# A masked attention kernel: adjacency turned into saturated integer codes in place, and node order restored by strided accesses

## The reference

```
h      = maximum(layernorm(x), 0)
scores = where(adj > 0, (h @ weight) @ input.T, -2**32 + 1)
out    = x + softmax(scores / 0.07, axis=1) @ input
```

## Time and profile before

| What | Value |
|---|---|
| median of 3 runs | 926.37 us |
| span of the profiled execution, first to last instruction | 922.5 us |
| its own time | not given; the median is 3.9 us above the span |
| PE busy (matmul) | 906.1 us, 98% |
| PE weight loads | 659.9 us, 72% |
| DVE busy | 814.5 us, 88% |
| ACT busy | 744.0 us, 81% |
| POOL busy | 705.6 us, 76% |
| DMA | 242.46 MB, mean 263 GB/s |
| issue to landing, median | adjacency chunk 5.3 us, `pT_dma` 3.5 us |

### The profile page before, as it was taken

The page is one execution under the profiler, slowest core; times in us unless marked ns, Lnnn a source line. Parts: engine busy times, 40 slices in busy tenths (PEclk is TensorE's granted clock), DMA queues, the critical chain, the costliest instruction groups (busy, mean ns, idle before and its releaser), DMA issues.

```text
span 922.5 us, 26099 instructions
## 1 busy us (share of the span) xinstructions
PE 906.1 (98%) x7566; PEld 659.9 (72%) x7566; DVE 814.5 (88%) x1626; ACT 744.0 (81%) x1468; POOL 705.6 (76%) x587
## 2 busy tenths in 40 slices
PE   7989999999999999999999999999999999999997
PEld 4466777777777777777777777777777777777776
DVE  6998889988998899889988998898889888988985
ACT  5987888888888888888888888888888888888885
POOL 5999878787778877887788778877887788788712
PEclk9999999999999999999999999999999999999999
DMA  9789999999999999999999999999999999999965
GB/s 343 232 224 257 279 267 278 257 287 266 286 278 267 272 273 273 267 272 273 276 273 267 269 274 274 275 260 276 276 268 265 276 274 278 260 270 269 278 105 100
DMA packets 360361, 242.46 MB, mean 263 GB/s; under 512 B 321808, under 2 KB 340368, under 8 KB 341904
## 3 DMA queue, kind: packets, MB, share of 16 engines
q1 hardware_dynamic: 353136, 238.87, 100.9%
q10 hardware_dynamic: 7200, 3.28, 1.5%
HBM read 160.50 MB, written 3.15 MB: 177 GB/s over the span
## 4 chain that ended last, share of the span: by engine, by line
PE 93%; DVE 2%; DMA 2%; SPq 2%; issue 1%; ACT 0%; DVEq 0%; ACTq 0%
PE ps_s L900 38%; PE ps_o L948 26%; PE ps_o L950 13%; PE ps_t L923 13%; DMA pT_dma<-split 2%; SPq L353 1%; PE ps_t L967 1%; DVE probs L695 1%; PE ps_s L977 1%; DMA nodes_raw<-in_L_gnn_input_dram 0%; DVE v L763 0%; DVE pT_lo L718 0%; DVE split L724 0%; PE ps_o L967 0%; DVE pT_hi L714 0%
## 5 line engine op out<-in xcount | busy, mean ns | idle before, releaser
L695 DVE CUSTOM_DVE_ANT_0 probs<-ps_s,absent 128x1024 f32<-128x1024 f32 x288 | 351.4, 1220 | 49.6 <-PE ps_s L900 42.8
L900 PE MATMUL ps_s<-yT_hi,hT 128*128 128x512 f16 x1152 | 389.2, 379 | 1.0 <-DVE chunk_max L695 0.9
L460 POOL TENSOR_SCALAR absent<-present 128x2048 bf16<-128x2048 bf16 x141 | 294.3, 2087 | 34.9 <-POOL present L451 34.3
L587 ACT ACTIVATE pT_hi<-ps_t 128x512 f16<-128x512 f32 x281 | 167.7, 597 | 156.0 <-PE ps_t L923 155.9
L451 POOL TENSOR_SCALAR present<-adj_i 128x2048 bf16<-128x2048 int32 x144 | 273.6, 1900 | 13.3 <-DMA adj_i<-in_adj_dram 13.3
L948 PE MATMUL ps_o<-v,pT_dma 128*128 128x256 f16 x1152 | 222.1, 273 | 5.2 <-DMA pT_dma<-split 2.9
L557 ACT ACTIVATE ps_t<-probs,neg_max,exp_scale 128x512 f32<-128x512 f32 x285 | 220.3, 773 | 2.6 <-DVE neg_max L705 1.2
L900 PE MATMUL ps_s<-yT_lo,hT 128*128 128x512 f16 x576 | 218.3, 379 | 0.0
L718 DVE TENSOR_TENSOR pT_lo<-ps_t,pT_hi 128x512 f16<-128x512 f32 x284 | 194.3, 684 | 21.8 <-ACT pT_hi L587 20.4
L948 PE MATMUL ps_o<-v,pT_hi 128*128 128x256 f16 x1152 | 205.9, 273 | 0.9 <-DVE pT_lo L718 0.8
L950 PE MATMUL ps_o<-v,pT_dma 128*128 128x128 f16 x1152 | 206.5, 220 | 0.0
(11 more groups left out here) (82 smaller groups left out, 508.8 us busy)
## 6 DMA issues: line engine op xcount, KB each, us to landing
adj_i<-in_adj_dram SPq DMA_DIRECT2D x144, 1024.0 KB, 5.3
pT_dma<-split SPq DMA_TRANSPOSE x288, 3.5
nodes_raw<-in_L_gnn_input_dram SPq DMA_DIRECT2D x6, 512.0 KB, 6.7
x_res<-in_x_dram SPq DMA_DIRECT2D x48, 64.0 KB, 3.9
out_dram<-fin ACTq DMA_DIRECT2D x48, 64.0 KB, 2.5
x_ln<-in_x_dram SPq DMA_DIRECT2D x46, 64.0 KB, 5.0
hT<-h_split SPq DMA_TRANSPOSE x45, 5.0
x_ln<-in_x_dram ACTq DMA_DIRECT2D x2, 64.0 KB, 3.0
```

Of the source, the lines that this page charges most:

```text
L460: nc.gpsimd.tensor_scalar(by_block(absent[:, c, :]), by_row(flags(s, c)), -ABSENT, ABSENT, ALU.mult, ALU.add).then_inc(absent_done, 1)
L587: nc.scalar.activation(pT_hi[:, p % BANKS, :], turn_area(k, at), ACT.Copy).then_inc(hi_done, 1)
L695: nc.vector.tensor_tensor_reduce(out=probs[:, s, j * SCORE:(j + 1) * SCORE], in0=ps_s[j % 2][:, :], in1=absent[:, c, part * SCORE:(part + ...
L900: made = nc.tensor.matmul(ps_s[j % 2][:, q * 512:(q + 1) * 512], hT[:, s, part, :], y[:, cols], start=(part == 0 and y is yT_hi), stop=(pa ...
```

## The change

The flags and `absent` go. One pass on GpSimd (`convert`) reads a chunk as int32 and writes it over itself as uint32: 2^39 - 2^40*adj, which saturates to the largest uint32 for no edge and to 0 for an edge. The mask subtracts these codes; the scales of h and y are lowered so that scores are small beside them. Since the pass is in place, adjacency stays in the natural order of nodes, and so do scores and `probs`. The block order that `v` needs is restored elsewhere: `nodesT` is written with a step of 4 fp32 elements (16 bytes), and TensorE's transposes (as weights), `exp_d` and `split_d` read `probs` with that step.

A chunk's buffer is now free only when its last mask is done, so each load waits for `masked`. For tile 1, chunks 0 and 1 have a buffer of their own, `adj_x`, and are loaded at the start.

```diff
-    H_SCALE = 2.0 ** 12
-    Y_TOP = 14
+    H_SCALE = 2.0 ** -3
+    Y_TOP = 3
...
-    ABSENT = 2.0 ** 64
+    PRESENT_STEP = -2.0 ** 40
+    ABSENT = 2.0 ** 39
...
-        absent = sb("absent", [P, CONVS, CONV], bf16)
-        present = sb("present", [P, 2, CONV], bf16)
+        adj_x = sb("adj_x", [P, 2, CONV], int32)
...
-        def by_block(part):
-            return part.rearrange("q (g b p) -> q g b p", b=PER_TURN, p=P)
-        def by_row(part):
-            return part.rearrange("q (g p b) -> q g b p", b=PER_TURN, p=P)
+        def adjacency(u, c):
+            return adj_x[:, c, :] if isinstance(u, int) and u == 1 and c < 2 else adj_i[:, c, :]
+        def codes(u, c):
+            return adjacency(u, c).bitcast(uint32)
+        def by_row(turn):
+            return turn.rearrange("q (p b) -> q b p", b=PER_TURN)
+        def by_block(turn):
+            return turn.rearrange("q (b p) -> q b p", b=PER_TURN)
...
             def load_adj(u, c):
-                sp.dma_start(adj_i[:, c, :], adj_v[u][:, c * CONV:(c + 1) * CONV]).then_inc(adj_in[c], 16)
+                landed = adj_x_in[c] if isinstance(u, int) and u == 1 and c < 2 else adj_in[c]
+                sp.dma_start(adjacency(u, c), adj_v[u][:, c * CONV:(c + 1) * CONV]).then_inc(landed, 16)
+
+            def next_adj(u, c):
+                sp.wait_ge(masked, u * SCORES + (PER_CONV * (c + 1) - SCORES * (2 if isinstance(u, int) and u == 2 and c < 2 else 1)))
+                load_adj(u, c)
...
             sp.dma_start(x_res[:, 0, :], x_v[0]).then_inc(x_res_in[0], 16)
+            for c in range(2):
+                load_adj(1, c)
             for u in range(2, 4):
                 sp.wait_ge(h_done, u - 1)
                 load_x(u, u % 2)
-            def early_adj(n):
-                sp.wait_ge(present_done, n + 1)
-                load_adj(n // CONVS + 1, n % CONVS)
-            for n in range(2 * CONVS - 1):
-                early_adj(n)
+            next_adj(1, 2)
+            for c in range(2):
+                next_adj(2, c)
...
                     turn_d(t, 2, g, late(at, 0, g) if at == LAST else evac(t, g - 2))
-                next_adj(0)
+                if has(at, 2):
+                    next_adj(t + 2, 2)
                 for g in range(2):
                     turn_d(t, 4, g, late(at, 1, g) if at == LAST else evac(t, 2 + g))
-                next_adj(1)
...
+                if has(at, 3):
+                    next_adj(t + 3, 0)
                 if has(at, 1):
                     for g in range(2):
                         turn_d(t + 1, 0, g, late(at, 2, g) if at == LAST - 1 else evac(t, 6 + g))
-                next_adj(2)
...
                     sp.dma_start(x_res[:, s, :], x_v[t + 1]).then_inc(x_res_in[s], 16)
+                if has(at, 3):
+                    next_adj(t + 3, 1)
...
-            def find_present(u, s, c):
...
-                nc.gpsimd.tensor_scalar(flags(s, c), adj_i[:, c, :], 1.0, 0.0, ALU.min, ALU.max)\
-                    .then_inc(present_done, 1)
...
-                nc.gpsimd.tensor_scalar(by_block(absent[:, c, :]), by_row(flags(s, c)), -ABSENT, ABSENT,
-                                        ALU.mult, ALU.add).then_inc(absent_done, 1)
...
+            def convert(u, c):
+                if isinstance(u, int) and u == 1 and c < 2:
+                    pool.wait_ge(adj_x_in[c], 16)
+                else:
+                    pool.wait_ge(adj_in[c], u * 16 + (0 if c < 2 and not (isinstance(u, int) and u == 0) else 16))
+                pool.sem_inc(pool_waited, 1)
+                nc.gpsimd.tensor_scalar(codes(u, c), adjacency(u, c), PRESENT_STEP, ABSENT, ALU.mult, ALU.add)\
+                    .then_inc(coded, 1)
...
-                nc.gpsimd.tensor_scalar(split[:, d, 0, :], part, 1.0, 1.0, ALU.mult, ALU.mult)\
+                nc.gpsimd.tensor_scalar(by_block(split[:, d, 0, :]), by_row(part), 1.0, 1.0, ALU.mult, ALU.mult)\
...
-                nc.scalar.activation(part if n is None else ps_t[n % BANKS][:, :], part, ACT.Exp,
+                nc.scalar.activation(part if n is None else by_block(ps_t[n % BANKS][:, :]),
+                                     part if n is None else by_row(part), ACT.Exp,
...
-            def early_absent(u, c):
...
-                nc.scalar.activation(nodesT[:, k * TURN:(k + 1) * TURN], nodes_bank[k % 2], ACT.Copy)\
+                nc.scalar.activation(by_row(nodesT[:, k * TURN:(k + 1) * TURN]), by_block(nodes_bank[k % 2]), ACT.Copy)\
...
+                dve.wait_ge(coded, u * CONVS + (c + 1))
...
-                    in0=ps_s[j % 2][:, :], in1=absent[:, c, part * SCORE:(part + 1) * SCORE],
+                    in0=ps_s[j % 2][:, :], in1=codes(u, c)[:, part * SCORE:(part + 1) * SCORE],
...
+                rows = by_row(probs[:, par, (k + 2) * TURN:(k + 3) * TURN])
                 for b in range(PER_TURN):
-                    col = (k + 2) * TURN + b * P
-                    made = nc.tensor.transpose(area[:, b * P:(b + 1) * P], probs[:, par, col:col + P],
-                                               ident[:, :])
+                    made = nc.tensor.transpose(area[:, b * P:(b + 1) * P], rows[:, b, :], ident[:, :])
```

More of the change, by code:

```diff
@@ L21, in gnn_masked_attention_kernel @@
     fp32 = mybir.dt.float32
-    bf16 = mybir.dt.bfloat16
     fp16 = mybir.dt.float16
     int32 = mybir.dt.int32
+    uint32 = mybir.dt.uint32
     ALU = mybir.AluOpType
@@ L135, in gnn_masked_attention_kernel @@
         minus_half = sb("minus_half", [P, 1], fp32)
-        absent_top = sb("absent_top", [P, 1], fp32)
         stats = sb("stats", [P, 2, 6], fp32)
@@ L184, in gnn_masked_attention_kernel @@
         adj_in = [sem(f"adj_in{i}") for i in range(CONVS)]
+        adj_x_in = [sem(f"adj_x_in{i}") for i in range(2)]
         stored = [sem(f"stored{i}") for i in range(2)]
@@ L188, in gnn_masked_attention_kernel @@
         half_done = sem("half_done")
[L189 to L192, removed]
+        coded = sem("coded")
         stats_done = sem("stats_done")
@@ L495, in _ @@
             for c in range(CONVS):
-                if c == 2:
-                    pool.wait_ge(absent_done, 1)
-                convert(0, 0, c, False)
-            pool.wait_ge(absent_done, 2)
-            find_present(1, 1, 0)
-            pool.wait_ge(absent_done, 3)
-            find_present(1, 1, 1)
-            make_absent(1, 1, 0, True)
+                convert(0, c)
+            for c in range(2):
+                convert(1, c)
             v_lo_pool(0)
-            pool.wait_ge(absent_done, 4)
-            find_present(1, 1, 2)
-            make_absent(1, 1, 2, True)
+            convert(1, 2)
             make_h(2, 0)
-            find_present(2, 0, 0)
+            convert(2, 0)
             v_lo_pool(1)
-            find_present(2, 0, 1)
+            convert(2, 1)
             v_lo_pool(2)
@@ L518, in step @@
                     if at != 0:
-                        convert(t + 2, par, 1, True)
+                        convert(t + 2, 1)
                 if has(at, 3):
@@ L523, in step @@
                 if has(at, 2):
-                    convert(t + 2, par, 2, True)
+                    convert(t + 2, 2)
                 if has(at, 3):
-                    convert(t + 3, 1 - par, 0, True)
+                    convert(t + 3, 0)
                 if at == LAST - 1:
@@ L593, in y_hi @@
                                      scale=y_scale).then_inc(y_hi_done, 1)
-            def early_absent(u, c):
-                act.wait_ge(present_done, u * CONVS + c + 1)
-                act.wait_ge(masked, u * SCORES + (PER_CONV * (c + 1) - SCORES))
-                nc.scalar.activation(by_block(absent[:, c, :]), by_row(present[:, (u + c) % 2, :]), ACT.Identity,
-                                     bias=absent_top[:, :], scale=-ABSENT).then_inc(absent_early_done, 1)
             for u in range(2):
@@ L633, in step @@
                 for z in range(CYCLES):
-                    if at == 0 and z > 0:
-                        early_absent(2, z - 1)
                     hi_p(t, CYCLE * z, at)
@@ L685, in mask @@
                 c = j // PER_CONV
-                if isinstance(u, int) and (u, c) in ((1, 1), (2, 0), (2, 1)):
-                    dve.wait_ge(absent_early_done, u + (1 if (u, c) == (2, 1) else 0))
-                elif isinstance(u, int) and u < 2:
-                    dve.wait_ge(absent_done, u * CONVS + c + (0 if (u, c) == (1, 2) else 1))
-                else:
-                    dve.wait_ge(absent_done, u * CONVS + (c - 2))
+                dve.wait_ge(coded, u * CONVS + (c + 1))
                 dve.wait_ge(scores_made, u * SCORES + (j + 1))
```

27 lines of the change are left out of this document (1 added, 26 removed).

## The result

The changed kernel takes 1028.4 us, the median of 4 runs (1027.6 to 1035.5), beside 926.2 for the kernel before on the same chip: 1.1126 times the time, 95% interval 1.109 to 1.116. That is 102 us slower. It lies inside the range of 926 to 1056, but the likeliest time, 932, is 96 us off. That the range held the result is luck.

What follows compares the result with a forecast made beforehand. PE, busy for all 18.42 us of a period, was taken as the bound. Span 922.5 + 4.1 + 1.0 + 0.5 + 0.2 + 0.2 = 928.5, plus 3.9 to the median, gave 932 us; 8-of-10 range 926 to 1056.

Steps and rivals of the forecast that it cites:

- The DMA order in the loop: SP's queue in the loop: pairs of transposes behind loads still land in time, slack 1.5 and 1.1 us; 0, narrowly.
- Rival (b): Loop: transposes by DMA land late, 0.5 us per third, 69 us, to 1001; chance 0.08 including mixtures.
- The weights' step: TensorE's transposes reading probs as weights at a 16-byte step: no cost, hidden behind the moving operand; taken as 0.
- Rival (a): TensorE's transposes: the stepped weight load sets the pace, 0.105 us more each, 121 us, to 1053; chance 0.30.
- ACT: Loop: stepped exp_d reads up to 0.43 us longer, ACT at most 17.7 of 18.42 us; 0, by narrow cover.
- The node copies: Prologue, ACT's 12 stepped writes of nodesT: between 0 and 5 us, taken as 0.5 us.
- GpSimd: Two passes per chunk become one of 2.0 us; busy time falls some 280 us, near 420; 0 on the time.
- The mask: DVE's mask with a 4-byte instead of 2-byte second operand: still 1220 ns, no change.
- The prologue: Three loads ahead of the first transposes: PE waits 4.1 us more, plus 1.0 for lower clock and second wait.
- The likeliest case's own range: Whole kernel: bounds of the forecast's own terms around 932, given as 927 to 942 us.
- the second wait: PE's prologue wait of 2.26 us ending at 52.22, which may shrink as DVE's v products catch up.
- What would show it: Profile signs: period 18.4 us, four transposes in 0.61 us or about 0.93, no PE waits for pT_dma in the loop.

Runs made afterwards that it cites:

- experiment 5: The kernel before, with only the loop's adjacency loads waiting for the mask and issued right ahead of the pairs of transposes: 1043.5 us, ratio 1.1275.
- experiment 6: The changed kernel, with each loop load of adjacency issued between the two transposes of a pair, steps kept: 1018.1 us, ratio 1.097.
- experiment 3: The kernel before, with the 16-byte step in TensorE's transposes (weights) alone: 947.8 us, ratio 1.0245.
- experiment 4: The kernel before, with the 16-byte step in exp_d alone: 926.2 us, ratio 1.0009.
- experiment 10: The changed kernel, steps kept, with loop loads issued behind the pairs and one load instead of three ahead of the first transposes: 952.4 us, ratio 1.031.
- experiment 8: The changed kernel without steps (nodes in natural order), loop loads behind the pairs, one load ahead of the first pair, x_ln before tile 1's loads: 926.4 us.
- experiment 1: The changed kernel, with transposes and exp_d reading contiguously instead of with 16-byte steps, same issue order: 1040.9 us, ratio 1.124.

## Why the prediction was right or wrong

**The DMA order in the loop, taken at 0 "narrowly": this is the step that failed,** and it is 71 of the 96 us missed. The prediction worked out when transfers move and land, and found a slack of 1.1 us. It left the issue of a pair at the 2.8 us of the earlier trace rows, whatever stands ahead. Close behind a load a pair takes 4.6 to 4.9 us on SP, which does nothing else meanwhile. The slack of 1.1 us was no cover for three times 1.9 us in one list, since the lateness stays in the list: a pair issued late makes the next load late, and that the next pair. Its sentence "a delay doesn't pile up" was the false one. The sign of it stood in the trace of before, in a place that the text looked at only for its products. SP's queue in the prologue of the kernel before, behind the earlier trace rows:

```profile
41.95 0.58 SPq L322 DMA_DIRECT2D adj_i<-in_adj_dram  x1
42.74 4.90 SPq L353 DMA_TRANSPOSE pT_dma<-split  x2
```

A load, a pair 0.8 us behind it, and 4.90 us to issue the pair, of which SP waited for nothing: the line of the operation in this stretch reads

```profile
L353 SPq DMA_TRANSPOSE pT_dma<-split x2: 1232/2365/3498, 42.7 to 44.1; - x2
```

It is the pattern that the change makes three times a period, priced in full, and pairs of over 4 us come in that trace up to 226 us (experiment 5). Three pairs at 4.9 with the rest of the list (1.2 + 0.4 + 0.4 + 3 x 0.35, and gaps of some 3 us as the changed kernel has them) are 20.7 us against PE's 18.4. Times 46 that is 106 us, for 71 measured. How much of the 71 is the long issue and how much the late landing is not shown. In the changed kernel SP waits for 1.8 us of 500, so there its list sets the period; experiment 6 loses nearly as much with short issues and landings of up to 7.2 us. Both come from a load close ahead of a transpose.

**Rival (b)** named late transposes in the loop and gave 69 us for them at a chance of 0.08. The 71.3 measured fit its number, but only half of its reasoning: late landings are there, 5.7 us for 3.4, but its half a microsecond was not worked out from any row, and it had no price for the issue. That the number fits is luck.

**The weights' step, taken at 0: wrong, 22.7 us** in experiment 3. The first of the two reasons, that the moving operand's pace of 0.107 us covers the load, was partly right: the load grew by 69 ns and the pace by 23. The second, the 10% of GpSimd's strided pass, carried no weight for another engine and half the step. Rival (a) had the mechanism, and its price of 121 us (119 by its own rows, since 0.213 less 0.11 is 0.103) was 5 times too high: a load at 210 ns sets 0.133 us and not 0.213. The Trainium skill's rule of 16-byte lines, in "Advanced Engine Details and Errata", SBUF Cachelines, is borne out in sign at three places (weight load 141 to 210 ns, `exp_d` 773 to 1277, node copies 597 to 1124); its factor, which the page does not give, is 1.5 to 1.9 here.

**ACT: right in the loop.** The bound of 0.43 us was passed (0.50), and the time was hidden all the same. Its "narrow cover" of 17.7 of 18.42 us, 96%, was measured at 95% in experiment 4. The node copies were taken at 0.5 us between 0 and 5; the first score product is 1.75 us later in experiment 10 than in 8, and before it PE waits for the copies for up to 0.83 us at a time, for 0.34 in 8.

**GpSimd: right.** 1906 ns for 2.0 forecast, 419 us busy for about 420, and worth nothing on the time (experiment 8).

**The mask: right,** 1219 ns for 1220.

**The prologue: right in mechanism and size.** 4.1 + 1.0 us forecast, 4.8 and 5.5 measured. PE waits 3.75 us where it waited 0.38, 3.4 more for 4.1, and the lower clock came behind it for some 3 us, as said. The product stands at 49.23 and not at 46.7, since the three loads went out later than the 35.5 forecast (SP's queue in the changed kernel):

```profile
37.84 1.28 SPq L328 DMA_DIRECT2D adj_i<-in_adj_dram  x3
```

From there the prediction's own steps (1.9, then 7.8 for three loads and 1.5 for a transpose) give 49.0. Of the 2.3 us by which the loads are late, 1.75 may be the node copies; the rest was not taken apart.

**The likeliest case's own range,** 927 to 942, does not follow from its terms. Added to 926.4, the wait of 4.1 alone gives 930.5, or 928.2 if the second wait of 2.26 went; all upper bounds together (4.1, 1.7, 5, 0.8 and 0.6) give 938.6.

**What would show it** worked as a test: the period is 20.0 and not 18.4, so the forecast was wrong; four transposes at 0.70 lie between its 0.61 and rival (a)'s 0.93; and PE's waits for `pT_dma` in the loop point to (b).

## What to carry to other kernels

Price the issue of a transfer as well as its landing: sum what the issuing engine spends per period with each issue as long as it is in the order that the change makes, and look through the whole trace, prologue included, for one place where that order already stands. A load that waits for a buffer belongs behind the urgent transfers that are ready at the same time; moving three lines of the list was worth 71 us here, more than the rest of the change cost. A layout that saves work on an engine off the path (some 286 us of GpSimd's time) and puts a step on the reads of the engine that is the bound loses: some 20 ns on each of 1152 transposes was 22.7 us.

## What the runs showed of the hardware that was not expected

- The issue of a DMA transpose is not of constant length. It takes 1.23 us where no load stands close ahead (median 1237 ns of the 164 from 250 to 750 us in the kernel before), and the second of two in a row, 0.7 to 1 us behind a 1 MB load, takes 2.8 to 3.5 us, up to 3.9 (1231/2680/3937 ns). With the loads on another queue there are slow issues too (1232/1387/3530 ns). A load between the two, as in experiment 6, leaves both at 1.23 us, and they land after up to 7.2 us instead of 4.4. What limit holds the second one was not found.
- Taking the steps out of the changed kernel made it 12 us slower (experiment 1), and the same order in the kernel before ended 15 us above the changed kernel (experiment 5). The cause of either is open.
- With 128 columns of 4 bytes and a step of 16, a weight load takes 1.5 times as long, yet the transposes' pace grows only by a fifth; ACT's read of 512 such elements costs 1.0 ns more for each.
